# Three rounded products instead of one fp32 product in the output projection of a transformer layer, with the weight's low half fetched into the context's tiles

## The reference

```python
result = tgt + merge(softmax(q @ k.T * scale, causal) @ v) @ sa_wproj + sa_bproj     # self-attention of layernorm(tgt)
xq = layernorm(result); xs = layernorm(src)                                          # src: the context, 750 x 512
k2, v2 = split(xs @ ed_wkv); q2 = xq @ ed_wq
result = result + merge(softmax(q2 @ k2.T * scale) @ v2) @ ed_wproj + ed_bproj       # the output projection: ed_wproj
result = result + relu(layernorm(tgt) @ ff_w1 + ff_b1) @ ff_w2 + ff_b2
```

## Time and profile before

| | |
|---|---|
| median of three runs | 1388.59 us |
| profiled execution, its own time | 1385.79 us |
| its span, first to last instruction | 1383.9 us |
| TensorE busy | 1318.9 us, 95% |
| VectorE, ScalarE, GpSimd busy | 787.0, 653.9, 683.7 us |
| mean granted TensorE clock | 0.985 of full speed |
| one batch of cross-attention | 82.5 us |

### The profile page before, as it was taken

The page is one execution under the profiler, slowest core; times in us unless marked ns, Lnnn a source line. Parts: engine busy times, 40 slices in busy tenths (PEclk is TensorE's granted clock), DMA queues, the critical chain, the costliest instruction groups (busy, mean ns, idle before and its releaser), DMA issues.

```text
span 1383.9 us, 24323 instructions
## 1 busy us (share of the span) xinstructions
PE 1318.9 (95%) x9129; PEld 1068.7 (77%) x9129; DVE 787.0 (57%) x2000; ACT 653.9 (47%) x1574; POOL 683.7 (49%) x549
## 2 busy tenths in 40 slices
PE   7999999999899999998799899999999999999998
PEld 6888888888788888886677687777877777787764
DVE  6613223242677676776565656657565665755565
ACT  5311101242656566655526356463655646356344
POOL 3232221232435466556654557575574756657451
PEclk9999999999899999999899899999999999999999
DMA  7400102114834566645288567566657557655641
GB/s 236 146 16 16 61 31 84 38 60 123 184 79 123 152 138 134 142 122 159 78 146 136 92 85 132 83 119 103 90 107 108 115 83 114 104 94 73 93 67 41
DMA packets 98263, 142.22 MB, mean 103 GB/s; under 512 B 9597, under 2 KB 62629, under 8 KB 98146
## 3 DMA queue, kind: packets, MB, share of 16 engines
q1 hardware_dynamic: 98146, 140.67, 50.3%
HBM read 59.40 MB, written 22.02 MB: 59 GB/s over the span
## 4 chain that ended last, share of the span: by engine, by line
PE 74%; ACT 6%; POOL 5%; DMA 5%; DVE 5%; issue 4%; SPq 1%; POOLq 0%; ACTq 0%; DVEq 0%
PE ps L1646 18%; PE ps L452 10%; PE ps L422 10%; PE ps L163 9%; PE ps_pair L1663 6%; PE ps L1678 5%; PE ps L1692 5%; PE ps L1746 4%; ACT ca_xT_f L1571 2%; DMA ctx_tokens<-in_ctx_dram 2%; ACT ca_xT L1568 1%; DMA sa_K_stack<-sa_rows 1%; ACT ca_probT L1532 1%; POOL sa_rows L156 1%; POOL sa_fin L1001 1%
## 5 line engine op out<-in xcount | busy, mean ns | idle before, releaser
L1513 POOL TENSOR_TENSOR ca_partial<-ca_partial,ca_probT 125x896 f32<-125x896 f32 x118 | 249.3, 2113 | 171.2 <-ACT ca_probT L1532 166.6
L1584 DVE TENSOR_REDUCE ca_maxes<-ps 112x1 f32<-112x375 f32 x512 | 253.9, 541 | 107.6 <-PE ps L1678 105.5
L1532 ACT ACTIVATE ca_probT<-ps_pair 125x448 f32<-125x448 f32 x384 | 211.8, 555 | 210.4 <-PE ps_pair L1663 209.2
L1678 PE MATMUL ps<-ca_k_stack,ca_q_stack 96*112 96x376 f32 x512 | 171.9, 365 | 12.7 <-DVE ca_maxes L1584 11.6
L311 POOL TENSOR_TENSOR ff_hT<-ff_hrelu,ff_hT 128x512 fp32r<-128x512 f32 (+1 forms) x64 | 77.8, 1217 | 203.2 <-DVE ff_hT L393 203.2
L1663 PEld LDWEIGHTS ps_pair<-ca_q_stack,ca_k_stack 98*125 98x125 f32 x768 | 131.3, 188 | 55.1 <-issue 43.9
L1663 PE MATMUL ps_pair<-ca_q_stack,ca_k_stack 98*125 98x224 f32 x768 | 164.2, 296 | 2.9 <-ACT ca_probT L1532 2.7
L1646 PE MATMUL ps<-ca_xT,w_a 128*128 128x376 f32 x768 | 155.9, 340 | 0.0
L422 PE MATMUL ps<-ff_w,ff_hT 128*128 128x512 f32 x672 | 155.5, 390 | 0.0
L1646 PE MATMUL ps<-w_b,ca_xT 128*125 128x512 f32 x576 | 150.2, 396 | 0.7 <-DVE sa_res L1128 0.5
L422 PEld LDWEIGHTS ps<-ff_w,ff_hT 128*128 128x128 f32 x672 | 125.6, 188 | 25.8
(11 more groups left out here) (138 smaller groups left out, 2361.4 us busy)
## 6 DMA issues: line engine op xcount, KB each, us to landing
ca_k_stack<-ca_keys SPq DMA_DIRECT2D x96, 376.0 KB, 8.0
sa_Q_stack<-sa_rows SPq DMA_DIRECT2D x96, 112.0 KB, 3.6
sa_K_stack<-sa_rows SPq DMA_DIRECT2D x96, 112.0 KB, 3.8
ca_q_stack<-q_out SPq DMA_DIRECT2D x96, 112.0 KB, 9.7
ctx_tokens<-in_ctx_dram SPq DMA_DIRECT2D x14, 750.0 KB
ctx_tokens<-in_L_xattn_ff_w_dram SPq DMA_DIRECT2D x16, 512.0 KB, 5.1
q_out<-sa_yT SPq DMA_DIRECT2D x16, 448.0 KB, 4.0
ff_xin<-in_x_dram SPq DMA_DIRECT2D x7, 512.0 KB, 3.8
```

Source lines behind the costliest of these rows:

```text
L1513: pool.tensor_tensor(total, total, half(a), ALU.add).then_inc(partial_done, 1)
L1532: act.activation(probT[u // GH][0:JT, u % GH].rearrange("p a t -> p (a t)"), ps_p[u % 2][0:JT, 0:2 * T], ACT.Exp).then_inc(exp_done, 1)
L1584: dve.tensor_reduce(maxes[:, q, j, a:a + 1], ps_s[n % 3][0:TQ, 0:JH], AX_X, ALU.max).then_inc(s_read, 1)
L1678: pe.matmul(ps_s[n % 3][0:TQ, 0:JP], q_stack[0:KS, h, TQ * q:TQ * (q + 1)], k_stack[0:KS, h, a, :], start=True, stop=True).then_inc(s_psum, 1)
```

## The change

The output projection becomes three rounded products. What that needs is made in these places:

- In self-attention, `ed_wproj` is loaded in two halves (slots 28 and 44), rounded by ScalarE, its rest taken by VectorE, and both stored to DRAM (`wp_out`), high and low. The early load of the next weights waits for that (slot 60 instead of 7).
- The high half takes `wp`'s place in SBUF. For the low half there is no room: `wp_lo` lies over the last four of the six context tiles. SP fetches it each batch at the end of g = 3 (item "weights_low"), behind the last transpose of the context, for batches 2 to 7.
- Both halves of E stand in g = 0 now, in (0,6), (0,7) and (0,9), (0,10). V's first product, which had (0,7) and (0,9), goes to (0,0) and (0,1).
- The next context may only come when E is through with `wp_lo`: its fetch is at (0,11), for batch b + 1, and waits for E. The statistics go to (1,8) to (2,1), the normalising to (2,4) to (2,10).
- The divided result goes to ring places of two halves (`oT`, five). ScalarE rounds it (`D_high`, slot 5), GpSimd takes the rest (`D_low`, slot 6), VectorE for the last four groups.

```diff
+OUTPUT_WEIGHTS = [28, 44]
...
-        if n == Y_WEIGHTS[-1] + 2:
+        for h in range(2):
+            if n == OUTPUT_WEIGHTS[h]:
+                items.append(("load_output", h))
+            if n == OUTPUT_WEIGHTS[h] + 8:
+                items.append(("round_output", h))
+                rests[n + 1].append(("keep_output", h))
+        if n == OUTPUT_WEIGHTS[1] + 16:
             items.append(("stage_next",))
...
-NORMALISE = (1, 3, 5, 7, 9, 10)
+NORMALISE = (4, 5, 6, 7, 9, 10)
...
-STATISTICS = ((0, 5), (0, 7), (0, 9), (0, 11), (1, 0), (1, 1))
+STATISTICS = ((1, 8), (1, 9), (1, 10), (1, 11), (2, 0), (2, 1))
+OFFSET = (2, 3)
...
-            put((0, 0, 1, 1), ("E", b - 2, 0), 0 <= b - 2 < B - 1)
+            put((0, 1), ("V", b, 0), now and b > 0)
             put((2, 3), ("K", s, 0), keys)
             put((4, 5), ("K", s, 1), keys)
-            put((7, 9), ("V", b, 0), now)
+            put((7, 9), ("V", b, 0), now and b == 0)
+            put((6, 6, 7, 7) if keys else (0, 0, 1, 1), ("E", b - 2, 0), 0 <= b - 2 < B - 1)
+            put((9, 9, 10, 10), ("E", b - 2, 1), 0 <= b - 2 < B - 2)
         elif g == 1:
...
-            put((6, 6, 7, 7), ("E", b - 2, 1), 0 <= b - 2 < B - 2)
...
-            if i == (3 if s <= NG else LAST_D) and 0 <= s - 4 < NG:
-                items.append(("D", s - 4))
+            divided = 3 if s <= NG else LAST_D
+            for j, name in enumerate(("D", "", "D_high", "D_low") if s <= NG else ("D", "D_high", "D_low")):
+                if name and i == divided + j and 0 <= s - 4 < NG:
+                    items.append((name, s - 4))
...
+                if (g, i) == (0, 11) and b > 0:
+                    items += [("context", b + 1, a) for a in range(2)]
-        if g == 3 and b + 2 < B:
-            items += [("context", b + 2, a) for a in range(2)]
+        if g == 3 and 1 <= b < B - 1:
+            items.append(("weights_low", b + 1))
...
+    def result_low(eng, G):
+        piece, full = oT[G % PIECES], oT_f32[G % PIECES]
+        for n, t in halves_of(G):
+            eng.wait_ge(ohi_done, n)
+            eng.tensor_tensor(piece[:, LO, t], full[:, t], piece[:, HI, t].bitcast(F32), ALU.subtract).then_inc(olo_done, 1)
...
+        if name == "weights_low":
+            b = item[1]
+            for a in range(2):
+                wait_acc_psum(sp, "T", b, KT - 1, a)
+            sp.dma_start(wp_lo[:].bitcast(F32), wp_out[LO]).then_inc(wp_lo_landed, 16)
...
         if name == "context":
             _, b, a = item
             wait_acc_psum(sp, "T", b - 1, KT - 1, a)
+            if b >= 3:
+                wait_acc_psum(sp, "E", b - 3, 1)
...
+        if name == "D_high":
+            G = item[1]
+            for n, t in halves_of(G):
+                act.wait_ge(o_read, n)
+                act.copy(oT[G % PIECES][:, HI, t], oT_f32[G % PIECES][:, t]).then_inc(ohi_done, 1)
...
-            mm = pe.matmul(acc[0:TQ, :], oT[b % 2][:, part, TQ * m:TQ * (m + 1)], wp[part],
-                           start=part == 0, stop=part == KT - 1)
+            for i, (o_half, w_half) in enumerate(PASSES):
+                mm = pe.matmul(acc[0:TQ, :], oT[(KT * b + part) % PIECES][:, o_half, TQ * m:TQ * (m + 1)], wp(w_half, part),
+                               start=(part, i) == (0, 0), stop=(part, i) == (KT - 1, len(PASSES) - 1))
```

More of the change, by code:

```diff
@@ L645, in plan_attention @@
     items[behind:behind] = [("ff", "last")]
-    return items + [("ca",) + o for o in other[start:]]
+    return items + [("ca",) + o for o in other[start:] if o not in early]
 class Stage:
@@ L1310, in plan_cross_attention @@
                     items.append(("statistics", b + 1, STATISTICS.index((g, i))))
-                if g == 1 and i == 9:
+                if (g, i) == OFFSET:
                     items.append(("offset", b + 1))
-                if g == 2 and i in NORMALISE:
-                    items.append(("normalise", b + 1, NORMALISE.index(i)))
-        if g == 3 and b + 2 < B:
-            items += [("context", b + 2, a) for a in range(2)]
+                if g == 2:
+                    items += [("normalise", b + 1, t) for t in range(CTX_TILES) if NORMALISE[t] == i]
+                if (g, i) == (0, 11) and b > 0:
+                    items += [("context", b + 1, a) for a in range(2)]
+        if g == 3 and 1 <= b < B - 1:
+            items.append(("weights_low", b + 1))
         if g == 1 and 0 <= b - 2 < B - 1:
@@ L1347, in cross_attention @@
     UNITS, SCORES, PAIRS, SUMS, XT = 12, 16, 3, 5, 8
+    PIECES = KT + 1
     def sem(name):
@@ L1353, in sb @@
         return at("ca_" + name, shape, dt, offset)
-    wp_tiles = [sb("wp_0", [P, 3, C], F32, 116736), sb("wp_3", [P, 1, C], F32, 36224)]
-    wp = [wp_tiles[k // 3][:, k % 3, :] for k in range(KT)]
+    wp_tiles = [sb("wp_0", [P, 3, C], F32R, 116096), sb("wp_3", [P, 1, C], F32R, 36224)]
     xs = ctx_tile[0:JT]
@@ L1404, in tokens, with wp, halves_of @@
         return a[b].rearrange("(t p) c -> p t c", p=TQ)
+    def wp(half, k):
+        return wp_lo[:, k] if half == LO else wp_tiles[k // 3][:, k % 3, :]
+    def halves_of(G):
+        parts = 2 if G == KT * B - 1 else 1
+        return [(G + i + 1, slice(T // parts * i, T // parts * (i + 1))) for i in range(parts)]
+    def result_low(eng, G):
[3 more added lines that the diff above has]
+            eng.tensor_tensor(piece[:, LO, t], full[:, t], piece[:, HI, t].bitcast(F32), ALU.subtract).then_inc(olo_done, 1)
     def context_low(eng, b, m, a):
@@ L1515, in gpsimd @@
             context_low(pool, *item[1:])
+        if name == "D_low" and item[1] < NG - KT:
+            result_low(pool, item[1])
         if name == "statistics" and item[2] == NT - 1:
@@ L1617, in vector @@
             b, g = G // KT, G % KT
-            if b >= 2 and g == 0:
-                wait_acc_psum(dve, "E", b - 2, 1)
+            if G >= PIECES and (g == 1 or G == PIECES):
+                wait_acc_psum(dve, "E", (G - PIECES) // KT, 1)
             if G == 0:
@@ L1622, in vector @@
                 dve.wait_ge(what, n * B)
-            parts = 2 if G == KT * B - 1 else 1
-            for i in range(parts):
-                t, total = slice(T // parts * i, T // parts * (i + 1)), slice(T + T // parts * i, T + T // parts * (i + 1))
-                dve.reciprocal(oT[b % 2][:, g, t], ps_o[:, total]).then_inc(inv_done, 1)
-                dve.wait_ge(inv_done, G + i + 1)
-                dve.tensor_tensor(oT[b % 2][:, g, t], ps_o[:, t], oT[b % 2][:, g, t], ALU.mult).then_inc(o_read, 1)
+            full = oT_f32[G % PIECES]
+            for n, t in halves_of(G):
+                dve.reciprocal(full[:, t], ps_o[:, T + t.start:T + t.stop]).then_inc(inv_done, 1)
+                dve.wait_ge(inv_done, n)
+                dve.tensor_tensor(full[:, t], ps_o[:, t], full[:, t], ALU.mult).then_inc(o_read, 1)
+        if name == "D_low" and item[1] >= NG - KT:
+            result_low(dve, item[1])
         if name == "K_rest":
```

68 lines of the change are left out of this document (52 added, 16 removed).

## The result

The changed kernel takes **1429.38 us** (median of four runs, 1427.82 to 1431.44), the kernel before 1387.24 beside it: ratio 1.0306, 95% interval 1.0288 to 1.0325. It is 42 us slower, where 1383 was forecast. The profiled execution took 1427.82 us, with a span of 1424.9.

The account below looks back on a forecast made before the run. TensorE, busy 1318.9 of 1383.9 us, was taken as the bound. Terms -9.0 - 7.5 + 8.0 + 2.2 + 0 + 1.0 - 1.7 + 1.8 = -5.2 us against the median 1388.6 gave 1383 us; range 1374 to 1394.

Parts of the forecast that it names:

- C: Statistics at (1,8) and key casts: later context fetch and late key stack make VectorE and ScalarE wait, +8.0 us.
- rival 1: (1,8) and key casts in (2,1): key stack slows the fetch to a third, both land late; 1402 us, chance 0.19.
- A: Output projection: three rounded matmuls replace one fp32, a pair of steps falls from 1.72 to 1.40 us; -9.0 us.
- Rival 3: g = 3 and g = 1: ScalarE or VectorE as long as TensorE, half of A arrives; about 1388 us, chance 0.15.
- B: Old context wait at (0,5) goes: 4.34 us in batch 1, 0.64 in each of batches 2 to 6; -7.5 us.
- D: Rounding of the divided result: covered except ScalarE's casts in six stages of g = 3 at 0.37 us; +2.2 us.
- E: Self-attention: casts, subtractions and transfers that make the weight's halves, mostly covered; +1.0 us, bounds 0 and 5.
- F: Batch 1: V's first product ahead of the keys fills TensorE's waits for exp of 0.64 and 1.07 us; -1.7 us.
- G: End of the kernel: last projection starts 1.4 us later behind new subtractions, three others on VectorE cost 0.4 each for two; +1.8 us.
- the low weight: Six fetches of 1 MB behind the last transpose, wanted in (0,6), land in time: 0, bound +1 us a batch.

Follow-up runs that it names:

- experiment 2: Changed kernel with each half of the context's fetch issued as 112 + 13 rows instead of 125: 1374.82 us, ratio 0.9909 to the kernel before.
- experiment 1: Changed kernel in which SP waits for the next context to land before issuing the key stack of g = 1 (batches 1 to 6): 1398.53 us, ratio 1.0094.
- experiment 6: Experiment 2 with the output projection as one fp32 product again, the weight's low part left out: 1384.5 us, 9.7 us over experiment 2.
- experiment 5: Kernel before the change, with each half of the context's fetch issued as 112 and 13 rows: 1382.1 us, ratio 0.9961.
- experiment 4: Changed kernel without the low weight's fetches and wait, low passes reading the high tile, context still late: 1426.62 us, ratio 1.0279.

## Why the prediction was wrong

**C is the step that failed.** M', the maxima's transposes of g = 1, stands at 1052.5 us in the changed kernel. The start of the fetch was right: asked for 4.3 us ahead of M', moving from M' - 2.9 (forecast - 3). The wanted time was nearly right: VectorE was ready at 1072.23 - 6.45 = 1065.78, M' + 13.3 (forecast + 12.3). Wrong was "so the last third of the fetch runs at half speed or less", priced at half: what was left ran at 34%, at 26% beside the key stack and then beside the query stack, which C does not name. It was also somewhat more than a third: 42%, because the first ten packets took 1.5 us. At half speed these 104 packets would have landed by about M' + 15, within the bound of + 16; the context was there at M' + 19.7 instead of + 12.5. The share of 1.02 at only 130 GB/s in the earlier trace rows had held the price. Sixteen engines busy with a stack move no more than five with a context, so a busy engine is there three times slower, and a transfer on five of them gets the time of five slow engines. I read the row as "all engines are taken" and halved. At a third, the last third of 12 us would have come out at M' + 5 + 12 = M' + 17, not the M' + 16 of rival 1.

**The clock was left out of C.** I had seen in the earlier trace rows that a stall of this size is followed by 6.8 us at 1.2 GHz, and booked it as a gain not counted. A stall of 6 us in each of five batches, and of 8.9 in batch 1, brings it six times: in the changed kernel each of the six has its stretch at 1.2 GHz of 6.8 to 10.2 us, with a loss of 1.8 us where I worked it out above.

C as forecast was + 8.0 us. What its waits cost can be read from the stages of the changed kernel and of experiment 2: the six stages g = 1 are longer by 52.6 us, 41.6 of them in batches 2 to 6 and the rest in batch 1 (30.6 against 19.6). The medians differ by 54.6.

**Rival 1 named place and mechanism, but its second half did not come.** It put the wait at (1,8) with the key stack as the cause, at 0.19 and 1393 to 1402 us, and the measured time is 27 us above that. The price was too small for the reasons above. The late casts of keys in (2,1) did not follow: in the changed kernel ScalarE waits for the key stack three times, 8.3 us in all, and g = 2 is 19.5 us. That TensorE's stop in g = 1 gives the stack this time back is likely, but no run separates it. Only where the stack itself was held back (experiment 1) did g = 2 grow.

**A, the products: right.** -9.0 forecast, 9.7 measured (experiment 6), and a pair of steps takes 1.40 us as the value projection does. The 24 pairs where TensorE is the chain are worth 7.7 us, as forecast. Rival 3 is out: neither ScalarE nor VectorE took the place of TensorE in g = 3 or g = 1 of experiment 2.

**B: nearly right in sum, wrong in its parts.** -7.5 forecast; the medians of experiment 5 give -4.9 (by the interval of the ratio -3.2 to -7.8). Its stages give -6.7, all in batch 1: the stall of 4.34 us and the slow clock behind it, which I had left out. The five waits of 0.64 us were worth nothing: with them gone, g = 0 is still 19.1 us. I had added up rows of a timeline without looking whether the stage gets shorter.

**D, E, F, G and the low weight: small, as forecast, but not one by one.** Stage g = 3 is 21.5 us (21.7 in the earlier trace rows); forecast was 21.4. From experiment 5 to experiment 2 a batch falls by 0.7 us (82.4 to 81.7), where the products are worth 1.3; so all small costs together take 0.6 a batch, and D had 0.37. The low weight is worth about 2.8 us in all (experiment 4), within its bound of 1 us a batch. The first M of cross-attention stands at 726.8 us, 725.2 before; in the kernels here with the same self-attention it stands anywhere from 723.9 to 729.3, so a cost of 1.0 us is neither shown nor excluded. At the end, E now starts 2.47 us behind the first division, 1416.08 to 1418.55, against 1.22 in the earlier trace rows: 1.25 us later, 1.4 forecast. F is not separated from the small costs: g = 3 of batch 0 and g = 0 of batch 1 take 37.4 us in experiment 2 and 39.1 in experiment 5, -1.7 as forecast.

**Taken together,** the forecast without C and its wait is -13.2 us, and the version without the wait (experiment 2) stands at -12.4. Much of that agreement is luck, as the stages of the profiled executions show. From g = 2 of batch 0 to g = 1 of batch 1 the forecast was -6.0 (B's 4.34 and F), and 8.7 us were gained (80.8 to 72.1). In the next six batches' worth of stages it was -8.7 (A -7.7, B -3.2, D + 2.2), and 4.3 were gained. For the end it was + 0.5 (A -1.3, G + 1.8), and 1.2 were gained. What lies ahead of the first M (+ 1.0 forecast) differs by up to 5 us between kernels with the same code there. What failed by tens of microseconds is one transfer's pace.

## What to carry to other kernels

When a transfer is moved, ask not only when it starts and how long it takes alone, but what is issued before it ends, and price the rest of it by what a busy engine moves in a stretch where all engines are busy: here a transfer on five of sixteen engines got 35 of 115 GB/s, five engines' part of what all moved. Look at the number of rows of every large transfer: 125 rows as 112 + 13 was one line, and turned a loss of 3.1% into a gain of 0.9%. And count a TensorE stall of some microseconds with the slow clock behind it, and a short wait only if the stage that holds it gets shorter.

## What the runs showed of the hardware that was not expected

A context packet from DRAM (6144 bytes) took 0.24 us alone and 0.85 beside the key stack, which copies inside SBUF; the stack's packets (3008 bytes) took 0.17 us on five engines and 0.42 to 0.43 on eleven to sixteen. On the five shared engines the stack's packets came behind those of the context, and on the other eleven the stack ran at once, so it is not the sharing of an engine that slowed the fetch, but something that the engines have in common. What that is, no run here tells. A limit of DRAM alone does not explain it: the same fetch on sixteen engines ran in a stretch of 214 GB/s (experiment 2).
